# Re-ordering the start of a four-layer residual chain: table loads, corner matrices and low-rank tables

## The chip, the cores and the metric

The kernel runs on one core of a Trainium2 chip. The metric is the device time of one execution in microseconds (us). The kernel before took 628.57 us, the median of three runs (627.66 to 631.0). Engines are named as the profile names them: PE is TensorE, PEld its weight loads, DVE VectorE, ACT ScalarE, POOL GpSimd, SP SyncE; ACTq and SPq are the instruction queues of ACT and SP, which issue DMAs and load registers.

## The reference

The input `x` has 8 batches of 256 tokens of 1024 features. Four residual layers follow each other (all float32):

```python
x = x + _L0_cond_ref(x, W0, b0, coeff, mask)      # x @ W0.T + b0 + coeff[b] * (x @ (2*mask[b]-1))
x = x + _L1_cond_ref(x, w1, scale_log, codebook, lora_A, lora_B)
        # delta = lora_B @ lora_A * 0.5;  n = (w1 + delta) / exp(scale_log) per group of 128 columns
        # q = nearest of 8 codebook levels (7 thresholds);  w_eff = q * scale + delta;  x @ w_eff.T
x = x + _L2_cond_ref(x, tok2, W2, b2, lora_As, lora_Bs)   # x @ W2.T + b2 + 2 * (x @ A[tok2[b]]) @ B[tok2[b]]
x = x + _L3_cond_ref(x, A3, B3, tok3)                     # (x @ B3[tok3[b]].T) @ A3[tok3[b]].T
```

Layers 1 and 2 are linear and the same for every batch, so the kernel multiplies their matrices once: P = (I + W1_eff)^T (I + W2)^T. The low-rank parts become small matrices: V = (I + W2)^T B3^T, and tables G that hold, per batch, the rows that close the product.

## The kernel before

The work has two parts. The first, up to about 232 us, builds P; the second runs eight batches with it. Every float32 matrix is split into a high and a low part (`_hi`, `_lo`, type fp32r), and a product is three matmuls: hi by hi, hi by lo, lo by hi. ACT writes the high part out of PSUM, DVE subtracts it to give the low part.

**Preparation.** SP loads W2 in eight row blocks (`w2n`, line 248). DVE adds the unit matrix to each (`w2_eye`, L795), PE transposes the blocks (L1013), ACT and DVE split them (L536 and L802). After each block PE adds that block's part of V (`v_part`, L1021) into the banks of delta1. Then come the transposes of B2, the small product of B3 and B2 (L1059, L1060), the transposes of A3 (L1066), and the correction of the G tables (L1073, and on DVE L841, L848, L850). POOL does two gathers and the sums of the quantiser.

**Table loads.** The tables of layers 2 and 3 are picked by token numbers. SP runs a loop of eight (L251 to L253): load the number from DRAM into a register, issue a DMA. ACT does the same eight times in its own program (`load_a3`, L523 and L524), two of them ahead of the first scaling of W1.

**Quantisation and P, in eight groups.** A group is 128 columns of W1 in two halves of 128x512. Each half goes through:

- `add_delta` on DVE (L732): raw weight plus the PE product delta (L982);
- `norm` on ACT (L487): division by the scale;
- `terms` on DVE (L740 seven times and L759 once): seven comparisons;
- `sums` on POOL (L405 four times and L407): adding up the comparisons;
- `scaled` on ACT (L473), `effective` on DVE (L771), the split `w1_hi` on ACT (L494) and `w1_lo` on DVE (L775).

PE then computes the group's rows of P: eight steps t, each with three column pieces n (512, 512 and 256 columns) of three matmuls (L1122 to L1124). ACT and DVE split the result (`p_hi` L504 and L509, `p_lo` L785 and L789). In group g, DVE does `terms(g+1,1)`, `add_delta(g+2,0)`, `effective(g+1,0)`, `w1_lo(g+1,0)`, `add_delta(g+2,1)`, `terms(g+2,0)`, `effective(g+1,1)`, `p_lo(g)`, `w1_lo(g+1,1)`. The order on each engine is that of its program; nothing re-orders it. PE also transposes a block of W0 in each group (L998), whose unit matrix POOL has added (L413), and SP stores it.

**Batches.** From about 236 us on, PE runs layer 0 (L1156 to L1158) and the product with P (L1174 to L1176) for the eight batches.

## Time and profile before

| quantity | value |
|---|---|
| median of three runs | 628.57 us (627.66 to 631.0) |
| span of the profiled execution | 627.8 us |
| PE busy in the span | 579.3 us (92%) |
| DVE busy | 403.0 us (64%) |
| ACT busy | 285.2 us (45%) |
| POOL busy | 139.5 us (22%) |
| mean granted TensorE clock | 0.973 of full |

The three runs are timed apart from the profiled execution. Its own time is known only as its span, from the first instruction to the last; the median lies 0.8 us above it. A time in the rows is counted from the start of the span. In the windows each engine's figure is busy time in that stretch, and PEclk is the granted clock as a share of 2.4 GHz.

### The profile page before, as it was taken

Reading aid. Unit: us, or ns where it says so; the run is one execution under the profiler, and the core shown is the slowest. Engines: PE = TensorE matmul, PEld = TensorE weight load, DVE = VectorE, ACT = ScalarE, POOL = GpSimd, SP = SyncE. Lnnn points to the kernel's source line nnn. Section 1 sums busy time; section 2 is a strip of 40 time slices with the busy share of each in tenths; the row PEclk is TensorE's granted clock in tenths of the full one; section 3 lists DMA queues with packets and bytes.
Section 4 is the critical chain, followed back from the end, with each engine's and each line's share of the span. In section 5 each row is a group of like instructions: output and inputs, shape, how many; then the busy total and the mean of one; then the engine's idle time right before and its main releaser. Section 6 shows DMA issues by size and latency. Waiting matters only on the chain.

```text
span 627.8 us, 10523 instructions
## 1 busy us (share of the span) xinstructions
PE 579.3 (92%) x3636; PEld 523.5 (83%) x3636; DVE 403.0 (64%) x591; ACT 285.2 (45%) x535; POOL 139.5 (22%) x133
## 2 busy tenths in 40 slices
PE   5478869988997999999999999999999999999997
PEld 4478658877886889889989989989989988988986
DVE  5585997999999367476466456555646637547621
ACT  1325544344533376555365455455544635545520
POOL 2350576878777210000000000000000000000000
PEclk9579998998998999999999999999999999999999
DMA  8751344133310898128126325414604703803301
GB/s 247 183 94 18 35 135 140 63 100 100 100 33 34 278 351 275 69 101 290 46 101 218 116 96 166 173 57 164 214 33 138 263 19 127 286 3 131 105 1 67
DMA packets 60791, 81.12 MB, mean 129 GB/s; under 512 B 24992, under 2 KB 41376, under 8 KB 60768
## 3 DMA queue, kind: packets, MB, share of 16 engines
q1 hardware_dynamic: 51872, 79.23, 38.6%
q10 hardware_dynamic: 8608, 0.53, 0.9%
q0 software_dynamic: 288, 1.05, 0.4%
q8 instruction: 14, 0.23, 0.2%
q14 instruction: 9, 0.07, 0.0%
HBM read 66.12 MB, written 14.68 MB: 129 GB/s over the span
## 4 chain that ended last, share of the span: by engine, by line
PE 72%; DVE 10%; DMA 6%; issue 4%; ACT 3%; ACTq 2%; SPq 2%; DVEq 0%; POOL 0%; POOLq 0%
PE delta L1174 9%; PE delta L1176 9%; PE delta L1175 9%; PE bank L1156 7%; PE bank L1158 7%; PE bank L1157 7%; PE bank L1122 3%; PE bank L1123 2%; PE bank L1124 2%; PE delta L1158 2%; PE delta L1157 2%; PE delta L1156 2%; ACTq L523 2%; DVE term_b L740 2%; DMA g_dram<-a_lo 2%
## 5 line engine op out<-in xcount | busy, mean ns | idle before, releaser
L609 ACT CAST m_hi<-merged_ring 128x512 fp32r<-128x512 f32 x128 | 77.2, 618 | 86.9 <-PE delta L1158 33.0
L1156 PE MATMUL bank<-x_t_hi,m_hi 128*128 128x256 f32 x384 | 108.8, 283 | 1.9 <-DVE C_lo L789 1.2
L896 DVE TENSOR_TENSOR m_lo<-merged_ring,m_hi 128x512 fp32r<-128x512 f32 x128 | 84.7, 689 | 37.8 <-ACT m_hi L609 37.8
L1158 PE MATMUL bank<-x_t_hi,m_lo 128*128 128x256 f32 x384 | 108.7, 283 | 0.0
L1157 PE MATMUL bank<-x_t_lo,m_hi 128*128 128x256 f32 x384 | 108.7, 283 | 0.0
L1174 PE MATMUL delta<-P_hi,x_t_hi 128*128 128x512 f32 x256 | 101.8, 398 | 0.0
L1176 PE MATMUL delta<-P_hi,x_t_lo 128*128 128x512 f32 x256 | 99.9, 390 | 0.0
L1175 PE MATMUL delta<-P_lo,x_t_hi 128*128 128x512 f32 x256 | 99.8, 390 | 0.0
L890 DVE TENSOR_TENSOR merged_ring<-merged_ring,w_t 128x1024 f32<-128x1024 f32 x64 | 77.1, 1223 | 31.2 <-ACT merged_ring L599 26.3
L599 ACT ACTIVATE merged_ring<-mask_ring,batch_now 128x1024 f32<-128x1024 int32 x64 | 78.0, 1240 | 16.3 <-DMA mask_ring<-in_mask_Bx4096x_ik 15.4
L447 POOL CAST c_batch<-C_hi 128x256 fp32r (+1 forms) x24 | 9.6, 435 | 339.5 <-PE delta L1183 321.1
L1122 PE MATMUL bank<-w_hi 128*128 128x512 f32 (+1 forms) x192 | 72.4, 377 | 6.0 <-DVE P_lo L785 4.8
L1156 PEld LDWEIGHTS bank<-x_t_hi,m_hi 128*128 128x128 f32 x384 | 73.7, 192 | 2.5 <-DVE C_lo L789 1.4
L1157 PEld LDWEIGHTS bank<-x_t_lo,m_hi 128*128 128x128 f32 x384 | 73.7, 192 | 0.3
L1158 PEld LDWEIGHTS bank<-x_t_hi,m_lo 128*128 128x128 f32 x384 | 73.7, 192 | 0.0
L1123 PE MATMUL bank<-w_lo,w_hi 128*128 128x512 f32 (+1 forms) x192 | 69.8, 363 | 0.0
L1124 PE MATMUL bank<-w_hi,w_lo 128*128 128x512 f32 (+1 forms) x192 | 69.5, 362 | 0.0
L405 POOL TENSOR_TENSOR pooled<-pooled,term_b 128x512 f32<-128x512 f32 x32 | 49.1, 1535 | 59.5 <-DVE term_b L740 58.0
L1176 PEld LDWEIGHTS delta<-P_hi,x_t_lo 128*128 128x128 f32 x256 | 48.1, 188 | 10.4
L1175 PEld LDWEIGHTS delta<-P_lo,x_t_hi 128*128 128x128 f32 x256 | 48.2, 188 | 9.0
L1174 PEld LDWEIGHTS delta<-P_hi,x_t_hi 128*128 128x128 f32 x256 | 48.1, 188 | 9.0
L1122 PEld LDWEIGHTS bank<-w_hi 128*128 128x128 f32 x192 | 37.5, 195 | 12.5 <-issue 6.7
(139 smaller groups left out, 995.0 us busy)
## 6 DMA issues: line engine op xcount, KB each, us to landing
mask_ring<-in_mask_Bx4096x_ik SPq DMA_DIRECT2D x64, 512.0 KB, 4.3
w_nat<-in_L_cond_W SPq DMA_DIRECT2D x16, 512.0 KB, 5.4
x_nat<-in_x SPq DMA_DIRECT2D x8, 1024.0 KB, 6.7
out<-out_staged SPq DMA_DIRECT2D x32, 256.0 KB, 2.0
w_raw<-in_L_cond_weight SPq DMA_DIRECT2D x16, 256.0 KB, 3.0
w0t_dram<-w_out SPq DMA_DIRECT2D x8, 512.0 KB, 3.0
w_t<-w0t_dram SPq DMA_DIRECT2D x8, 512.0 KB, 4.8
g_batch<-g_dram SPq DMA_DIRECT2D x32, 128.0 KB, 3.7
```

The lines of the kernel that those rows point to most:

```text
L599: nc.scalar.activation(ring_f[:, k % MR], ring_i[:, k % MR], ACT.Identity, bias=now[:, 1:2], scale=now[:, 0:1]).then_inc(s["s_set"], 1)
L609: nc.scalar.copy(Mh[:, n % MR], ring_f[:, k % MR, h * HALF:(h + 1) * HALF]).then_inc(s["h_set"], 1)
L896: nc.vector.tensor_tensor(Ml[:, n % MR], ring_f[:, k % MR, h * HALF:(h + 1) * HALF], Mh[:, n % MR].bitcast(F32), ALU.subtract).then_inc(s[ ...
L1122: mm(o, W1h[:, t], Wh[:, t, c0:c1], start=(t == 0), stop=False)
L1123: mm(o, W1h[:, t], Wl[:, t, c0:c1], start=False, stop=False)
L1124: ins = mm(o, W1l[:, t], Wh[:, t, c0:c1], start=False, stop=(t == KT - 1))
L1156: mm(dst, mh, xTh[:, k], start=(k == 0 and o % 2 == 0), stop=False, skip_group_check=True)
L1157: mm(dst, mh, xTl[:, k], start=False, stop=False, skip_group_check=True)
L1158: ins = mm(dst, ml, xTh[:, k], start=False, stop=(k == KT - 1), skip_group_check=True)
L1174: mm(o, x1h[:, k, toks], Ph[:, k, cols], start=(k == 0), stop=False)
L1175: mm(o, x1h[:, k, toks], Pl[:, k, cols], start=False, stop=False)
L1176: mm(o, x1l[:, k, toks], Ph[:, k, cols], start=False, stop=False)
```

## The change

The change leaves the batches as they are and rewrites the first part.

- SP loads codebook and scales first, and the wait between W2 blocks 1 and 2 is gone. All sixteen table loads stand on SP in straight code, after the second W1 block and the first W0 block; the token number is read from the SBUF tile `tok` (before: from DRAM). They stand ahead of `raw_next(0, 2, h)`, the third W1 block.
- The unit matrices of W2 are added by POOL; those of W0 are a matmul of `ident` by `ident` on PE. POOL also makes the low part of A2 (`Wl[..D:D+NBR]`) and the low parts of the G tables.
- V no longer sits in the delta banks but in banks 7 and 2, and comes after the 512-column pieces n = 0 and 1 of group 0. Piece 2 of group 0 follows V. The transposes of W2 use three banks in turn instead of four.
- W1 of groups 0 and 2 is split into buffers of its own (`W1h_early`, `W1l_early`), so that `w1_hi` of groups 1 and 2 waits for less.
- The work for A3 and the G tables moves behind group 1 on PE (`tables()`), and behind `terms(3,1)` on DVE (`gsum`).
- The first three group bodies are written out by hand on DVE, ACT and PE, and the hardware loops over groups become straight code.

On DVE, ahead of the hardware loop of groups, the rows of the kernel before are these (`b_nat` is the B2 table, `a_nat` A2, `a_t` A3 transposed, `w_norm` the normed half of W1):

```order
L740 TENSOR_SCALAR term_d<-w_norm,thresholds,steps 128x512
L740 TENSOR_SCALAR term_b<-w_norm,thresholds,steps 128x512
L841 TENSOR_TENSOR b_nat<-b_nat,bank 128x512
L845 TENSOR_TENSOR w_lo<-a_nat,w_hi 128x8x128
L841 TENSOR_TENSOR b_nat<-b_nat,bank 128x512
L848 TENSOR_TENSOR a_lo<-a_t,a_hi 128x1024
L850 SCALAR_TENSOR_TENSOR ga_lo<-b_nat,ga_hi 128x1024
L873 UNCONDITIONAL_BRANCH
```

The terms above it are `terms(1,0)`. In the changed kernel only the two sums on `b_nat` are left on DVE, three groups later, behind `p_lo(1)` and `terms(3,1)`:

```order
L821 TENSOR_TENSOR P_lo<-bank,P_hi 128x512 x2
L825 TENSOR_TENSOR C_lo<-bank,C_hi 128x256
L763 TENSOR_SCALAR acc<-w_norm,thresholds,steps 128x512
L763 TENSOR_SCALAR term_a<-w_norm,thresholds,steps 128x512
L763 TENSOR_SCALAR pooled<-w_norm,thresholds,steps 128x512
L763 TENSOR_SCALAR term_b<-w_norm,thresholds,steps 128x512
L787 SCALAR_TENSOR_TENSOR acc<-acc,codebook_rows,term_a 128x512
L763 TENSOR_SCALAR term_c<-w_norm,thresholds,steps 128x512
L763 TENSOR_SCALAR term_d<-w_norm,thresholds,steps 128x512
L763 TENSOR_SCALAR term_b<-w_norm,thresholds,steps 128x512
L892 SCALAR_TENSOR_TENSOR b_nat<-b_nat,bank 128x512 x2
```

On PE the two products that feed these sums stand ahead of group 0 in the kernel before (`a_t` by `b_b_t`, L1073):

```order
L1066 MATMUL bank<-ident,a_nat 128x128 x8
L1073 MATMUL bank<-a_t,b_b_t 128x512 x2
L989 MATMUL delta<-ident 128x128
L982 MATMUL delta<-lora_a,lora_b_t 128x128 x8
L1122 MATMUL bank<-w_hi 128x512
```

In the changed kernel they stand between groups 1 and 2, and group 2 (the rows with `w_hi_early`) is behind them; the second product waits for the first sum on DVE:

```order
L1112 MATMUL bank<-w_hi,w_lo 128x256
L1153 MATMUL bank<-ident,a_nat 128x128 x8
L1161 MATMUL bank<-a_t,b_b_t 128x512 x2
L1028 MATMUL delta<-ident 128x128
L1021 MATMUL delta<-lora_a,lora_b_t 128x128 x8
L1110 MATMUL bank<-w_hi,w_hi_early 128x512
```

The diff, cut to its core:

```diff
 # sync
+            for h in range(2):
+                raw_next(0, 1, h)      # (b2c and the first block of W0 follow)
+            sp.wait_ge(s["tok_in"], 32)
+            for b in range(NB):
+                slot = sp.value_load(tok[0:1, 0, b:b + 1], min_val=0, max_val=a2.shape[0] - 1)
+                sp.dma_start(a2n[:, :, b, :], a2_rows[bass.ds(slot, 1)]...).then_inc(s["a2_in"], 16)
+            for b in range(NB):
+                slot = sp.value_load(tok[0:1, 1, b:b + 1], min_val=0, max_val=a3.shape[0] - 1)
+                sp.dma_start(a3n[:, :, b, :], a3_rows[bass.ds(slot, 1)]...).then_inc(s["a3_in"], 16)
+            for h in range(2):
+                raw_next(0, 2, h)
...
+            group(0, True, True)
             sp.wait_ge(s["y_set"], 1)
...
+            group(1, True, True)
+            group(2, True, True)
             sp.wait_ge(s["ga_hi"], 2)      # store of the G tables
 # gpsimd
+            for t in range(5):
+                w2_eye(t)
+            sums(0, 0)
+            for t in range(5, KT):
+                w2_eye(t)
+            sums(0, 1)
+            pool.wait_ge(s["ab_hi"], 1)
+            nc.gpsimd.tensor_tensor(Wl[:, :, D:D + NBR], a2n..., Wh[:, :, D:D + NBR]..., ALU.subtract)
             sums(1, 0)
+            group(0, 2)
+            group(1, 2)
+            group(2, 2)
+            pool.wait_ge(s["ga_hi"], 1)
+            nc.gpsimd.tensor_tensor(a3l[:, :], a3t[:, :], a3h..., ALU.subtract)
+            pool.wait_ge(s["ga_hi"], 2)
+            nc.gpsimd.tensor_tensor(gal[:, :], b2n[:, :], gah..., ALU.subtract)
 # scalar
-            for b in range(W2_FIRST):
-                load_a3(b)
             act.wait_ge(s["scale_set"], 1)
             for h in range(2):
                 norm(0, h, first=True)
...
+            w1_hi(2, 0)
+            p_hi(0, range(2))
+            w0_evac(0, 0, first=True)
+            p_hi(0, range(2, 3))
+            norm(3, 1)
+            w0_evac(0, 1, first=True)
+            scaled(2, 1)
+            w0_evac(1, 0)
+            w1_hi(2, 1)
+            w0_evac(1, 1)
+            p_hi(1)
+            a3_set(0)
 # vector
+            terms_a(0, 0, first=True, reused=False)   # four comparisons
+            w2_lo(0)
+            terms_b(0, 0)                             # the other four instructions
+            w2_lo(1)
...
+            w2_lo(7)
+            w1_lo(0, 1)
+            terms(1, 0)
+            terms(1, 1)
+            add_delta(2, 0, 0)
+            effective(1, 0, 1)
+            w1_lo(1, 0)
+            add_delta(2, 1, 0)
+            terms(2, 0)
+            effective(1, 1, 1)
+            w1_lo(1, 1)
+            v_lo(0)
+            terms(2, 1)
+            v_lo(1)
+            add_delta(3, 0, 1)
+            effective(2, 0, 0)
+            w1_lo(2, 0)
+            add_delta(3, 1, 1)
+            p_lo(0, range(2))
+            dve.wait_ge(s["bb_done"], 1)              # then b3b2 and y_col
+            terms_a(3, 0)
+            p_lo(0, range(2, 3))
+            terms_b(3, 0)
+            effective(2, 1, 0)
+            w1_lo(2, 1)
+            p_lo(1)
+            def group(g, par, quant, tables=False):
                 if quant:
                     terms(g + 1, 1)
+                if tables:                            # g == 2
+                    for h in range(2):
+                        gsum(h)
 # tensor
+            pe.wait_ge(s["w2_lo"], 2 * KT)
+            for n in range(2):
+                for t in range(KT):
+                    comp(n, t, *w1_split(0))          # pieces 0 and 1 of group 0
+            for k in range(HT):
+                v_part(k)
+            eye(2, 0)
+            delta(3, 1)
+            for k in range(HT, KT):
+                v_part(k)
+            pe.wait_ge(s["v_lo"], 1)                  # then the product of B3 and B2
+            pe.wait_ge(s["v_lo"], 2)
+            pe.wait_ge(s["ab_lo"], 1)
+            for t in range(KT):
+                comp(2, t, *w1_split(0))
+            pe.wait_ge(s["b3b2_set"], 1)
+            w0_transpose(0, 0, first=True)            # then group 1
+            tables()
+            def tables():
+                ...                                   # eight transposes of A3
+                for h in range(2):
+                    if h == 0:
+                        pe.wait_ge(s["a3_set"], 2)
+                    else:
+                        pe.wait_ge(s["gsum_set"], 1)
+                    mm(bank[MISC][:, :], b3b2[:, :], a3t[:, h * 512:(h + 1) * 512], start=True, stop=True)
```

## Rows read from the trace of the kernel before

**Rows 1.** Windows: stretch, its length, busy us (instructions) by engine, PEclk, DMA share, GB/s.

```profile
93.30:98.40 5.10, 5.07 (x18) 4.52 (x19) 4.97 (x9) 2.52 (x8) 3.30 (x3) 0.50 0.78 243
133.20:153.00 19.80, 17.04 (x98) 14.82 (x98) 18.43 (x26) 8.64 (x25) 15.43 (x12) 1.00 0.25 80
232.00:627.80 395.80, 391.83 (x2555) 358.42 (x2553) 221.94 (x319) 190.17 (x293) 10.03 (x28) 1.00 0.38 132
```

**Rows 2.** Chain that ended last, `effective` on DVE in two groups: start, us.

```profile
133.17 0.67 DVE acc L771
...
153.04 0.69 DVE acc L771
```

**Rows 3.** Timeline of PE, group 3: start, us, operation, idle before and releaser.

```profile
129.81 0.39 PE L989 MATMUL delta<-ident 128*128 128x128 f32 x2
...
133.90 1.16 PE L982 MATMUL delta<-lora_a,lora_b_t 128*128 x8 [2.82 <-DVE acc L771]
134.82 0.47 PE L1122 MATMUL bank<-w_hi 128*128 128x512 f32 x1
...
149.66 0.39 PE L989 MATMUL delta<-ident 128*128 128x128 f32 x2
```

**Rows 4.** Timeline of ACT before the first scaling.

```profile
14.09 6.93 ACTq L524 DMA_DIRECT2D a_nat<-in_L_cond_A  x2
...
21.36 2.44 ACT L487 ACTIVATE w_norm<-w_norm,scale_recip_now 128x128 f32<-128x128 f32 x8
```

**Rows 5.** Timeline of DVE in the preparation.

```profile
12.03 1.27 DVE L732 TENSOR_TENSOR w_norm<-w_raw,delta 128x512 f32<-128x512 f32 x2
...
22.67 0.55 DVE L740 TENSOR_SCALAR acc<-w_norm,thresholds,steps 128x512 f32<-128x512 f32 x1 [8.09 <-ACT w_norm L487]
...
31.20 2.47 DVE L802 TENSOR_TENSOR w_lo<-bank,w_hi 128x512 fp32r<-128x512 f32 x4
33.60 0.53 DVE L740 TENSOR_SCALAR acc<-w_norm,thresholds,steps 128x512 f32<-128x512 f32 x1
...
39.35 1.55 DVE L795 TENSOR_TENSOR w_nat<-w_nat,ident 128x128 f32<-128x128 f32 x2
...
64.30 0.54 DVE L740 TENSOR_SCALAR acc<-w_norm,thresholds,steps 128x512 f32<-128x512 f32 x1
```

**Rows 6.** Timeline of DVE, steady groups.

```profile
133.77 1.28 DVE L785 TENSOR_TENSOR P_lo<-bank,P_hi 128x512 f32 x2
...
136.40 1.32 DVE L740 TENSOR_SCALAR acc<-w_norm,thresholds,steps 128x512 f32<-128x512 f32 x1
...
143.14 0.68 DVE L732 TENSOR_TENSOR w_norm<-w_raw,delta 128x512 f32<-128x512 f32 x1
...
145.68 0.69 DVE L775 TENSOR_TENSOR w_lo<-acc,w_hi 128x512 fp32r<-128x512 f32 x1 [1.26 <-ACT w_hi L494]
```

**Rows 7.** Timeline of DVE: comparison c with POOL idle, then with POOL adding.

```profile
99.00 0.53 DVE L740 TENSOR_SCALAR term_c<-w_norm,thresholds,steps 128x512 f32<-128x512 f32 x1
...
109.98 1.51 DVE L740 TENSOR_SCALAR term_c<-w_norm,thresholds,steps 128x512 f32<-128x512 f32 x1
```

**Rows 8.** POOL's sums (L405), all: min/median/max ns.

```profile
L405 POOL TENSOR_TENSOR pooled<-pooled,term_d x16: 1261/1336/1367, 28.4 to 202.9; 128x512 f32<-128x512 f32 x16
```

**Rows 9.** Table loads on SP (L252, L253), ns.

```profile
L252 SPq TENSOR_LOAD <-in_itok_B_ptr x8: 930/1032/1837, 12.2 to 38.2; - x8
L252 SPq TENSOR_LOAD <-in_itok_B x8: 473/514/915, 14.2 to 39.4; - x8
L253 SPq DMA_DIRECT2D a_nat<-in_L_cond_lora_As x8: 387/389/3810, 15.7 to 40.4; - x8
```

**Rows 10.** Timeline of PE: V in the preparation; after its longest wait in the groups.

```profile
26.74 5.63 PE L1021 MATMUL delta<-b_t,w_nat 128*128 128x128 f32 x32 [7.76 <-ACT b_t L541]
...
93.33 2.05 PE L982 MATMUL delta<-lora_a,lora_b_t 128*128 128x128 f32 x8 [5.42 <-DVE acc L771]
```

**Rows 11.** Loads of W0 blocks 1 to 7 on SP (L290).

```profile
DMA to landing us min/median/max: 3.5/4.0/5.6
```

More of the change, by code:

```diff
@@ L547, in _ @@
-            for h in range(2):
-                act.wait_ge(s["prep_done"], V0 + h + 1)
-                nc.scalar.copy(Wh[:, h * HT:(h + 1) * HT, D + NBR:EXT], bank[VBANK[h]][:, :]).then_inc(s["prep_hi"], 1)
-            for h in range(2):
-                act.wait_ge(s["prep_done"], B2T0 + h + 1)
-                nc.scalar.copy(b2t[:, h * HT:(h + 1) * HT, :], bank[0 + h][:, :]).then_inc(s["prep_hi"], 1)
-            scaled(0, 1, first=True)
-            for h in range(2):
-                w1_hi(0, h, first=True)
@@ L557, in _ @@
-            for h in range(2):
-                norm(1, h)
-            for h in range(2):
-                act.wait_ge(s["prep_done"], A3T0 + h + 1)
-                nc.scalar.copy(a3t[:, h * 512:(h + 1) * 512], bank[h][:, :]).then_inc(s["prep_hi"], 1)
+            w2_hi(0)
+            w2_hi(1)
+            b3_set(0)
+            w2_hi(2)
+            b3_set(1)
+            w2_hi(3)
+            b2_set(0)
+            w2_hi(4)
+            scaled(0, 0, first=True)
+            b2_set(1)
+            w2_hi(5)
@@ L572, in group, with v_hi, a3_set @@
-            def group(g, quant, first=False):
+            def v_hi(h):
+                act.wait_ge(s["v_done"], h + 1)
+                nc.scalar.copy(Wh[:, h * HT:(h + 1) * HT, D + NBR:EXT], bank[VBANK[h]][:, :]).then_inc(s["v_hi"], 1)
+            def a3_set(h):
+                act.wait_ge(s["a3_tr"], h + 1)
+                nc.scalar.copy(a3t[:, h * 512:(h + 1) * 512], bank[MISC][:, :]).then_inc(s["a3_set"], 1)
+            scaled(1, 0)
+            norm(2, 0)
+            w1_hi(1, 0)
+            norm(2, 1)
@@ new lines, in _, with group @@
+            scaled(1, 1)
+            w1_hi(1, 1)
+            v_hi(0)
+            scaled(2, 0)
+            v_hi(1)
+            norm(3, 0)
+            w1_hi(2, 0)
[10 more added lines that the diff above has]
+            a3_set(0)
+            def group(g, quant, tables=False):
@@ L581, in group @@
                     norm(g + 2, 1)
+                if tables:
+                    act.wait_ge(s["gsum_set"], 2)
+                    nc.scalar.copy(gah[:, :], b2n[:, :]).then_inc(s["ga_hi"], 1)
                 if quant:
                     scaled(g + 1, 1)
-                w0_evac(g, 1, first)
-                p_hi(g, first)
+                w0_evac(g, 1)
+                p_hi(g)
                 if quant:
                     w1_hi(g + 1, 1)
-            group(0, 2, first=True)
-            group(1, 2)
-            with act.Fori(1, (G - 2) // 2) as j:
-                group(2 * j, 2)
-                group(2 * j + 1, 2)
+            for g in range(2, G - 2):
+                group(g, 2, tables=(g == 2))
             group(G - 2, 1)
@@ L826, in _ @@
-            for h in range(2):
-                effective(0, h, 0)
-            for h in range(2):
-                w1_lo(0, h)
+            terms_a(0, 0, first=True, reused=False)
+            w2_lo(0)
+            terms_b(0, 0)
+            w2_lo(1)
+            terms_a(0, 1, reused=False)
+            w2_lo(2)
+            terms_b(0, 1)
+            w2_lo(3)
+            w2_lo(4)
+            effective(0, 0, 0)
+            w2_lo(5)
+            w1_lo(0, 0)
+            w2_lo(6)
             for h in range(2):
@@ L868, in group @@
                     w1_lo(g + 1, 1)
-            per = 2 * 2 * 2
-            pairs = (G - 2) // 2
-            start = step.n
-            with dve.Fori(0, pairs) as j:
-                step.rebase(start + j * per)
-                group(2 * j, 0, 2)
-                group(2 * j + 1, 1, 2)
-                assert step.n == per, step.n
-            step.rebase(start + pairs * per)
+            for g in range(2, G - 2):
+                group(g, g % 2, 2, tables=(g == 2))
             dve.wait_ge(s["late_in"], 32)
@@ L1027, in _, with b3_transpose @@
[L1027 to L1031 removed]
+                        ins = nc.tensor.transpose(bank[W2RING[i % 3]][:, j * P:(j + 1) * P], w2n[:, t, k * P:(k + 1) * P], ident[:, :])
+                    ins.then_inc(s["w2_tr"], 1)
+            def b3_transpose(h):
+                if h == 0:
+                    pe.wait_ge(s["b3_in"], 16)
+                else:
+                    pe.wait_ge(s["b3_set"], 1)
@@ L1046, in _, with b2_transpose @@
-            pe.wait_ge(s["prep_lo"], 2 * KT)
-            for h in range(2):
+                    ins = nc.tensor.transpose(bank[MISC][:, t * P:(t + 1) * P], b3n[:, k * P:(k + 1) * P], ident[:, :])
+                ins.then_inc(s["b3_tr"], 1)
+            def b2_transpose(h):
+                if h == 0:
+                    pe.wait_ge(s["b2_in"], 16)
+                    pe.wait_ge(s["b3_set"], 2)
+                else:
+                    pe.wait_ge(s["b2_set"], 1)
                 for t in range(HT):
@@ L1087, in x_transpose, with group @@
                 ins.then_inc(s["t_done"], 1)
-            COLS = [(0, 512), (512, 1024), (1024, EXT)]
-            def group(g, par, quant, first=False, last=False):
+            def group(g, par, quant, last=False):
                 if quant:
```

420 lines of the change are left out of this document (197 added, 223 removed).

## The prediction

> **What bounds the kernel now.** I read the windows first, then the chain that ended last, then the timelines of PE, DVE, ACT and POOL up to 235 us, and at the end the queues. The windows show two regimes. From 232 us on PE is busy 391.8 of 395.8 us at full clock [rows 1]. The change does not touch this part, so it can only move its start. In a steady group, PE is busy 17.0 of 19.8 us and DVE 18.4. The chain agrees: `effective` of two groups lies at 133.17 and 153.04, 19.87 us apart, both pieces on DVE [rows 2], and PE stands 2.82 us before the delta of group 3 for exactly this DVE step [rows 3]. A group of PE work takes 149.66 - 134.82 = 14.8 us; a group of DVE work takes 19.9 us. So the groups are bound by DVE, in program order, and what counts is when DVE gets through the preparation, unless PE becomes late.
>
> The first comparison starts at 22.67, after 8.09 us of waiting for ACT [rows 5]. ACT could not scale because two table loads stood in front in its program (14.09 to 21.02); it scales from 21.36 [rows 4]. The terms of group 1 start at 64.30.
>
> **Part by part.** I follow DVE through the changed order, and PE where DVE has to wait for it. Times count from the span's start.
>
> *Step 1, the first comparison.* The first half of `add_delta` ends at 12.03 + 0.64 = 12.67. From the first scaling to the first comparison it took 22.67 - 21.36 = 1.3 us, and a small copy stands ahead (estimate 0.2). So terms(0,0) starts at about 14.2 instead of 22.67: 8.5 us earlier. The moved queue entries cost nothing here: codebook and scales come before the LoRA matrices, which land about 1 us later, and PE's first delta has that much room before DVE's chain of small operations is through.
>
> *Step 2, up to terms(1,0).* DVE has two passes of terms at 39.35 - 33.60 = 5.75 us each, 16 low parts of W2 at 2.47 / 4 = 0.62 (9.9), and six PSUM or split operations at 0.62 (3.7) [rows 5]. That is 25.1 us. The eight unit matrices are gone from DVE (one pair took 1.55). Each of the two splits of W1 waits for ACT 1.26 us [rows 6]: 2.5. So terms(1,0) starts at 14.2 + 25.1 + 2.5 = 41.8, against 64.30. In the kernel before V, its copies and the third transposes of PE lay between; they are now hidden behind terms of groups 1 and 2. The unit matrices on POOL delay its first sum, but W2 has landed by then; at worst they cost one POOL addition, 1.3 us [rows 8].
>
> *Step 3, up to the product of B3 and B2 being picked up (about 82.9).* Four passes of terms: 5.75 us when POOL rarely collides, 143.14 - 136.40 = 6.74 in a steady group [rows 6]. I take 6.5, since POOL is adding all the time: 26.0. POOL makes the low part of A2 ahead of sums(1,0): twice the size of a sum of 1.34, so 2.5 to 2.7 us in which the last comparison waits; I take 2.5 (none to 4 are the ends, since the DVE version in the kernel before was not in POOL's way). Four `add_delta`, three `effective`, three `w1_lo`, two `v_lo` at 0.62 and a pair of P_lo of 1.28: 8.7. Two waits for `w1_hi`: 2.5. The third, `w1_hi(2,0)`, waits for piece 2 of group 0, and that waits for V: after `effective(1,1)` PE does half a delta, 32 matmuls of V (5.63 us, partly at low clock, [rows 10]), the small product and half of piece 2, about 12 us, while DVE has 10.5 us to do. So 1.5 us. The sum is 41.2, and y_col is there at about 83.0.
>
> *Step 4, group 1 on PE.* It cannot start before that, because bank 7 holds the product. A transpose of W0 stands ahead (0.4), the group takes 14.8, the third piece waits for C_lo behind four comparisons (0.7), and step t = 3 needs the second block of W0, which is only requested after the second transpose: 0.4 + 4.0 us of landing [rows 11] against two steps of 1.8 us, so 0.8. It ends at about 99.9 (with the unit-matrix matmuls, 0.2, at 100.1). DVE has nothing left to do meanwhile: `p_lo(1)` stands in its order, and terms(3,1) is queued behind it. After ACT's 0.6 and 1.6 us of P_lo and C_lo, terms(3,1) starts at 102.3, with the sums of POOL long done, and takes about 6.3: 108.6.
>
> *Step 5, the G tables.* This is the wait the change adds. The second product of `tables()` waits for the first `gsum`, which DVE does after terms(3,1). Group 2 and all of PE is queued behind it. gsum 0.6, product 0.6: 109.8. PE stood for some 5 us. After a wait of 5.42 us the trace shows the next 5.1 us at a granted clock of 0.50, 1.2 GHz [rows 1, 10]. The delta then takes 1.7 us more to the first matmul of the group, and the group loses half of the remaining 3.4: 109.8 + 1.9 + 14.8 + 1.7 = 128.2. P_hi (0.6, of which 0.35 lies beside the last piece): P_lo(2) starts at 128.4.
>
> *Step 6, from there on.* Before, P_lo(2) started at 133.77 [rows 6]. The lead is 5.4 us. DVE would have been there at about 121, so PE is what is late. Afterwards DVE's 19.9 us per group bound again, and PE's 14.8 plus delta has room. POOL's a3l and gal (2.6 us each) fit into the gap before P_lo(2). The unit matrix of W0 leaves POOL: it touches one comparison per group, I take 0.15 us each, 0.5 in all; the extra unit matmuls in the last two groups, where PE bounds, give 0.3 back. Dynamic loops into straight code: the group before and after the loop's end have the same 19.9 us, so nothing. Sum: 5.6 us.
>
> The sum stands against the profiled execution of 627.8: 622.2. The median lies 0.8 above the span, so 628.57 - 5.6 = 623.0.
>
> *A rule against the change.* Comparison c took 0.53 us with POOL idle and 1.51 with POOL adding [rows 7]; the difference, 0.98, stays below one POOL addition (1.34). The Trainium skill (SBUF — State Buffer, "SBUF: two separate sides") says that VectorE and GpSimd share a port pair as an exclusive lock, held for a whole instruction; the trace agrees with 1.51 us. By that rule three subtractions of 1024 columns on POOL each hold DVE for up to 2.6 us, where DVE's own cost was 1.7 to 2.3, and the move would gain nothing. By the order above two of the three fall into DVE's gap.
>
> **Rivals.**
> *A longer lead (617.5).* Step 3 is pessimistic where POOL and DVE miss each other: with all six comparisons passes at 5.3 us (eight instructions, one collision instead of two) the passes save 4 x 1.2 + 2 x 0.45 = 5.7 us, and all of it reaches group 1 on PE. For it: sums(0,0) starts early. Against it: steady groups show 6.7.
> *Nothing left (627.5).* The lead is eaten by PE: group 1 also begins at 1.2 GHz (1.7), the second W0 block lands in 5.6 us instead of 4.0 (1.6) [rows 11], and the late A2 part holds DVE 1.3 more: 4.6 us, so 627.6. For it: PE stands before group 1 as well, for a few us.
> *Slower (641).* The sixteen table loads stand on SP ahead of the third W1 block, which `add_delta(2,0)` needs at 41.8 + 13.0 + 2.5 = 57.3. SP comes to them at about 15. The trace has no register load from SBUF. From below: a load of the value, 0.51, a DMA issue, 0.39, and register work of 0.6, 1.5 us each: done at 39. From above: the loop before took 12.2 to 40.8 for eight, 3.6 us each, with the pointer load of 1.03 and DMA issues up to 3.81 [rows 9]: done at 72.2, landed at 75.6, 18.3 us late, 641.3. It decides above (57.3 - 15 - 3.4) / 16 = 2.4 us per table. I take 1.5, since the pointer load is gone and W2 has landed after the first few.
> The Trainium skill (Runtime: NRT & Kernel Launch, "The ~15µs preamble/postamble breakdown") gives about 1.3 us for a register load from HBM; the trace shows 0.51 and 1.03. By 1.3 us a table costs 2.3, just inside.
>
> **How the numbers follow.** Forecast (620 to 626): 45%. Longer lead (613 to 620): 22%. Nothing left (626 to 630): 20%. Slower by the table loads: 8%. Other late steps adding up beyond 630: 5%. A measurement can tell about 0.5%, 3.1 us: faster is below 625.4, slower above 631.7. Faster: 22% and nine tenths of 45%, 0.63. Same: 0.22. Slower: 0.15. The range, 615 to 631, leaves out a part of the longer lead and the slower cases; the forecast's own range is 620 to 626.
>
> **What would show it.** First comparison near 14; terms(1,0) near 42; y_col near 83; PE with a wait of about 5 us before the second product of `a_t`, and PEclk 0.50 after it; P_lo(2) waiting for PE and starting near 128; later groups 19.9 us apart on DVE; layer 0 starting near 230. I am wrong if `add_delta(2,0)` waits for a DMA, if P_lo(2) does not wait for PE, or if DVE's period is no longer 19.9.

## The result and the profile after

The changed kernel takes 642.3 us (median of 5 runs, 638.0 to 642.6) against 628.7 of the kernel before: ratio 1.018, 95% interval 1.015 to 1.021. The whole interval lies above 1: it is slower, by 1.8%. I had forecast 623.0 us. The profiled execution is the quickest of the five (638.0, span 636.2). A later comparison gave the unaltered kernel 638.8 us (ratio 1.013, 1.007 to 1.019), so the loss is 10 to 14 us.

The windows after, columns as in [rows 1]:

```profile
90.00:108.70 18.70, 17.50 (x97) 14.53 (x98) 8.99 (x16) 7.57 (x20) 6.67 (x5) 1.00 0.58 128
108.70:135.40 26.70, 21.86 (x107) 17.69 (x108) 16.17 (x25) 9.72 (x24) 11.24 (x8) 0.87 0.21 67
135.40:158.60 23.20, 18.50 (x113) 16.24 (x112) 21.74 (x25) 9.39 (x27) 19.19 (x13) 0.98 0.33 106
178.40:198.30 19.90, 16.94 (x97) 14.48 (x96) 18.44 (x27) 8.64 (x25) 14.97 (x11) 1.00 0.16 54
240.00:636.00 396.00, 391.13 (x2547) 357.55 (x2545) 221.04 (x318) 189.40 (x292) 10.04 (x28) 1.00 0.38 132
```

In the batches PE is as busy as it was (391.1 of 396.0 us), and a steady group is still 19.9 us with 17 of PE and 18.4 of DVE. The loss lies in two stretches. Group 2 (108.7 to 135.4) takes 26.7 us with DVE busy only 16.2, so DVE waits there for 10.5. The next (135.4 to 158.6) takes 23.2 with DVE busy 21.7, so there DVE has more to do or does it more slowly.

The starts of the same steps in six kernels, from their timelines (us; `effective` and the P_lo of each group are on DVE; the four on the right are experiments of the next section):

| start of | before | after | g1 | g3 | h1 | i2 |
|---|---|---|---|---|---|---|
| effective(1,0) | 83.2 | 61.0 | 60.8 | 61.6 | 61.0 | 73.7 |
| P_lo(0) | 93.3 | 88.5 | 88.1 | 86.2 | 85.6 | 83.6 |
| P_lo(1) | 113.9 | 107.1 | 108.0 | 106.0 | 104.0 | 103.5 |
| P_lo(2) | 133.8 | 135.4 | 131.0 | 129.0 | 127.1 | 123.4 |
| P_lo(3) | 153.6 | 159.1 | 150.6 | 151.0 | 147.9 | 143.2 |
| P_lo(6) | 210.4 | 217.2 | 207.5 | 209.0 | 206.0 | 201.0 |
| P_lo(7) | 226.8 | 233.8 | 224.1 | 225.6 | 222.6 | 217.3 |
| span | 627.8 | 636.2 | 627.8 | 627.5 | 626.5 | 619.5 |

Read the first two columns downwards. The new order is 22.2 us ahead at effective(1,0), 4.8 at P_lo(0), 6.8 at P_lo(1), and then behind: 1.6, 5.5, 6.8, 7.0, and 8.4 in the span.

The timeline of PE after (start, us, operation, idle before and releaser) shows the first part of this:

```profile
56.07 7.30 PE L1082 MATMUL bank<-b_t,w_nat 128*128 128x128 f32 x64
...
71.01 2.08 PE L1021 MATMUL delta<-lora_a,lora_b_t 128*128 128x128 f32 x8 [5.32 <-DVE acc L803]
72.88 8.69 PE L1082 MATMUL bank<-b_t,w_nat 128*128 128x128 f32 x64
...
90.18 0.30 PE L1037 MATMUL bank<-ident,w_nat 128*128 128x128 f32 x1 [2.16 <-DVE b_b_t L880]
...
110.48 1.13 PE L1161 MATMUL bank<-a_t,b_b_t 128*128 128x512 f32 x2 [1.23 <-ACT a_t L568]
115.21 2.07 PE L1161 MATMUL bank<-a_t,b_b_t 128*128 128x512 f32 x2 [3.60 <-DVE b_nat L892]
```

Half of V is 32 matmuls in the code and stands here as x64. The row of before, x32 in 5.63 us, was therefore 16 matmuls and not the 32 that I read in it [rows 10]. The last row is the wait that the change adds: the second product of the tables, 3.60 us behind the first sum on DVE, and after it the clock has fallen:

```profile
115.20:120.20 5.00, 4.99 (x17) 3.96 (x18) 1.33 (x3) 0.00 (x0) 3.02 (x3) 0.50 0.00 0
```

The granted clock is 0.50, that is 1.2 GHz, for the 5 us from the product on, and the product takes 2.07 us where its twin took 1.13.

ACT and DVE in the same stretch, one fence each:

```profile
102.70 0.59 ACT L517 COPY w_out<-bank 128x512 f32<-128x512 f32 x1 [7.40 <-DMA w0t_dram<-w_out]
103.18 0.62 ACT L496 CAST w_hi_early<-acc 128x512 fp32r<-128x512 f32 x1
...
124.90 0.59 ACT L517 COPY w_out<-bank 128x512 f32<-128x512 f32 x1 [13.39 <-PE bank L1037]
125.38 0.21 ACT L483 COPY scale_recip_now<-scale_recip 128x8 f32<-128x8 f32 x1
125.62 1.28 ACT L488 ACTIVATE w_norm<-w_norm,scale_recip_now 128x128 f32<-128x128 f32 x4
126.81 0.61 ACT L496 CAST w_hi<-acc 128x512 fp32r<-128x512 f32 x1
```

```profile
117.32 0.69 DVE L892 SCALAR_TENSOR_TENSOR b_nat<-b_nat,bank 128x512 f32<-128x512 f32 x1 [2.16 <-PE bank L1161]
119.55 0.69 DVE L758 TENSOR_TENSOR w_norm<-w_raw,delta 128x512 f32<-128x512 f32 x1 [1.54 <-PE delta L1021]
120.16 0.68 DVE L803 TENSOR_TENSOR acc<-pooled,delta 128x512 f32<-128x512 f32 x1
127.45 0.69 DVE L808 TENSOR_TENSOR w_lo<-acc,w_hi 128x512 fp32r<-128x512 f32 x1 [6.61 <-ACT w_hi L496]
...
135.37 1.38 DVE L821 TENSOR_TENSOR P_lo<-bank,P_hi 128x512 fp32r<-128x512 f32 x2 [0.21 <-ACT P_hi L506]
...
139.04 2.61 DVE L763 TENSOR_SCALAR term_a<-w_norm,thresholds,steps 128x512 f32<-128x512 f32 x1
141.58 2.62 DVE L763 TENSOR_SCALAR pooled<-w_norm,thresholds,steps 128x512 f32<-128x512 f32 x1
144.12 0.53 DVE L763 TENSOR_SCALAR term_b<-w_norm,thresholds,steps 128x512 f32<-128x512 f32 x1
```

Twice ACT stands at the copy of a W0 column block, once for the store of the block before (7.40 us) and once for PE's transpose (13.39), and behind it in ACT's order stands the split of W1 for which DVE waits. The second time DVE stands for 6.61 us; with 2.16 at the second sum and 1.54 at `add_delta` that makes 10.3 of the 10.5 us. P_lo(2), where I had expected the wait, has 0.21: PE's group 2, which it needs, runs from the second product at 115.21 to 135.7 without a wait, so DVE and PE come to P_lo(2) at the same time. Then two comparisons take 2.6 us instead of 0.54; POOL's timeline has its two low parts exactly there:

```profile
138.80 2.57 POOL L432 TENSOR_TENSOR a_lo<-a_t,a_hi 128x1024 fp32r<-128x1024 f32 x1
141.34 2.58 POOL L434 TENSOR_TENSOR ga_lo<-b_nat,ga_hi 128x1024 fp32r<-128x1024 f32 x1
```

The table loads on SP did what they were meant to (16 loads in 18.3 us, answering to [rows 9]; the raw data of group 2 are asked for at 42.26):

```profile
23.94 8.68 SPq L252 DMA_DIRECT2D a_nat<-in_L_cond_lora_As  x8
33.41 8.81 SPq L255 DMA_DIRECT2D a_nat<-in_L_cond_A  x8
42.26 1.71 SPq L242 DMA_DIRECT2D w_raw<-in_L_cond_weight  x2
```

### The profile page after: what moved, and what is told of

The parts are those of the page before. It is cut to its first block, busy times and chain, and to the rows that moved or that the text cites. A ratio compares the mean times of both kernels' runs of the same rounds, so it can differ in the third digit from the quotient of the medians.

```text
span 636.2 us, 10123 instructions
## 1 busy us (share of the span) xinstructions
PE 585.6 (92%) x3652; PEld 527.0 (83%) x3652; DVE 401.7 (63%) x580; ACT 285.6 (45%) x535; POOL 143.3 (23%) x136
## 4 chain that ended last, share of the span: by engine, by line
PE 76%; DVE 11%; DMA 2%; ACT 2%; issue 1%; DVEq 0%; ACTq 0%
PE delta L1258 9%; PE delta L1260 9%; PE delta L1259 9%; PE bank L1240 7%; PE bank L1242 7%; PE bank L1241 7%; PE bank L1110 4%; PE bank L1112 3%; PE bank L1111 3%; PE delta L1242 2%; PE delta L1241 2%; PE delta L1240 2%; DVE term_b L763 2%; DVE term_c L763 1%; PE bank L1082 1%; PE delta L1267 1%
## 5 line engine op out<-in xcount | busy, mean ns | idle before, releaser
L1242 PE MATMUL bank<-x_t_hi,m_lo 128*128 128x256 f32 x384 | 108.7, 283 | 0.0
L1241 PE MATMUL bank<-x_t_lo,m_hi 128*128 128x256 f32 x384 | 108.7, 283 | 0.0
L625 ACT ACTIVATE merged_ring<-mask_ring,batch_now 128x1024 f32<-128x1024 int32 x64 | 77.9, 1239 | 19.2 <-DMA mask_ring<-in_mask_Bx4096x_ik 18.4
L1240 PEld LDWEIGHTS bank<-x_t_hi,m_hi 128*128 128x128 f32 x384 | 73.7, 192 | 3.9 <-DVE m_lo L934 2.3
L1241 PEld LDWEIGHTS bank<-x_t_lo,m_hi 128*128 128x128 f32 x384 | 73.7, 192 | 0.3
L1242 PEld LDWEIGHTS bank<-x_t_hi,m_lo 128*128 128x128 f32 x384 | 73.7, 192 | 0.0
L1110 PE MATMUL bank<-w_hi 128*128 128x512 f32 x144 | 55.0, 382 | 4.6 <-DVE P_lo L821 4.6
L406 POOL TENSOR_TENSOR pooled<-pooled,term_b 128x512 f32<-128x512 f32 x32 | 46.8, 1464 | 48.9 <-DVE term_b L763 46.2
L1260 PEld LDWEIGHTS delta<-P_hi,x_t_lo 128*128 128x128 f32 x256 | 48.0, 188 | 10.4
L1111 PE MATMUL bank<-w_lo,w_hi 128*128 128x512 f32 x144 | 52.9, 368 | 0.0
L1112 PE MATMUL bank<-w_hi,w_lo 128*128 128x512 f32 x144 | 52.8, 367 | 0.0
L959 DVE TENSOR_TENSOR out_staged<-delta,b_rows 128x512 f32<-128x512 f32 x32 | 21.4, 688 | 38.4 <-PE delta L1274 38.4
```

The lines of the kernel that those rows point to most:

```text
L625: nc.scalar.activation(ring_f[:, k % MR], ring_i[:, k % MR], ACT.Identity, bias=now[:, 1:2], scale=now[:, 0:1]).then_inc(s["s_set"], 1)
L1110: mm(o, hi[:, t], Wh[:, t, c0:c1], start=(t == 0), stop=False)
L1111: mm(o, hi[:, t], Wl[:, t, c0:c1], start=False, stop=False)
L1240: mm(dst, mh, xTh[:, k], start=(k == 0 and o % 2 == 0), stop=False, skip_group_check=True)
L1241: mm(dst, mh, xTl[:, k], start=False, stop=False, skip_group_check=True)
L1242: ins = mm(dst, ml, xTh[:, k], start=False, stop=(k == KT - 1), skip_group_check=True)
```

## The experiments

Each comparison ran beside the kernel before: 630.2 us in the first (e), 629.1 in the second (g), 628.7 in the third (h), 629.2 in the fourth (i). The changed kernel itself ran again only in the second (g0, 638.8 us); the e and h runs are set against it by their ratios. Marks such as P_lo(2) are those of one profiled execution each. The theory at the start: the loss is two waits by queue order in group 2 and the collision on POOL. The rivals: V is simply longer than I took it, or PE's clock is the limit.

**e1, the second product of the tables two tiles into group 2.**

```
-  (tables) wait gsum_set >= 1; matmul(b3b2, a3t[512:])
+  (group 2, t == 2) wait gsum_set >= 1; matmul(b3b2, a3t[512:])
   (as before)       wait gsum_set >= 2; transpose of W0
```

> The changed kernel with one edit: the second product of the G tables moves from the front of group 2 to just ahead of the first W0 transpose of group 2 (step t = 2), so PE does eye, delta and two steps of group 2 while DVE does terms(3,1). Theory A (that wait is what makes PE, then ACT and then DVE late): PE no longer stands 3.6 us at 115.2, w1_hi(3,0) no longer waits behind the W0 copy until 126.8, DVE's wait of 6.6 us before w1_lo(3,0) falls under 1, and P_lo(2) starts near 128 to 129 instead of 135.4: 6 to 7 us less, ratio to the kernel before about 1.008 (from 1.018). Theory B (PE is late anyway, by group 1 and by V before it, and the wait costs only itself): 2 us or less, ratio 1.015 or more.

636.0 us (631.0 to 639.5, 7 runs), ratio 1.009 (1.006 to 1.012). The wait of DVE at `w1_lo(3,0)` shrinks from 6.61 to 2.32 and P_lo(2) comes 5.5 us earlier:

```profile
121.94 0.69 DVE L808 TENSOR_TENSOR w_lo<-acc,w_hi 128x512 fp32r<-128x512 f32 x1 [2.32 <-ACT w_hi L496]
...
129.85 1.38 DVE L821 TENSOR_TENSOR P_lo<-bank,P_hi 128x512 fp32r<-128x512 f32 x2 [0.20 <-ACT P_hi L506]
```

The profiled execution is the fastest of the seven. In the medians the gain over g0 is smaller (ratio 1.009 against 1.013) and the intervals overlap; the same holds for e2.

**e2, the low parts of the G tables left out** (the high parts are stored twice).

```
-  gpsimd a3l = a3t - a3h (1024 columns), gal = b2n - gah (1024 columns)
+  gpsimd the same on 8 columns; store (gah, a3h) twice
```

> The changed kernel without the low parts of the G tables: POOL's two subtractions of 1024 columns are cut to 8 columns and the high parts are stored twice (this leaves part of the computation out). Theory A (each holds DVE's next comparison for a whole POOL instruction: term_a 2.61 and pooled 2.62 us at 139 instead of 0.54): 4.1 us less, all of it on the path since DVE bounds the groups from there on, ratio about 1.0115. Theory B (the stall only fills time that DVE would wait for PE or ACT): under 1 us, ratio 1.017 to 1.019.

635.0 us (633.1 to 641.6, 10 runs), ratio 1.010 (1.007 to 1.014). From P_lo(2) to P_lo(3) it is 19.6 us instead of 23.7, and comparison a is back at 0.53:

```profile
136.41 1.38 DVE L821 TENSOR_TENSOR P_lo<-bank,P_hi 128x512 fp32r<-128x512 f32 x2 [0.21 <-ACT P_hi L506]
...
140.10 0.53 DVE L763 TENSOR_SCALAR term_a<-w_norm,thresholds,steps 128x512 f32<-128x512 f32 x1
...
156.03 1.28 DVE L821 TENSOR_TENSOR P_lo<-bank,P_hi 128x512 fp32r<-128x512 f32 x2
```

**e3, V in one piece** ahead of `eye(2,0)` and `delta(3,1)`.

```
-  v_part(0..3); eye(2, 0); delta(3, 1); v_part(4..7)
+  v_part(0..7); eye(2, 0); delta(3, 1)
```

> The changed kernel with V computed in one piece: all eight v_part ahead of eye(2,0) and delta(3,1) on PE. Theory A (the second half of V, 8.7 us at half clock behind a delta that waits for DVE, sets piece 2 of group 0 and the pick-up of the B3-B2 product): V ends near 71, the waits of DVE at 82 (2.2 us) and 87 (3.2 us) go, y_col comes near 86 instead of 90, and 3 to 4 us reach the end, ratio about 1.012. Theory B (DVE's own passes of terms set y_col): under 1.5 us, ratio 1.016 or more.

638.7 us (637.2 to 639.9, 4 runs), ratio 1.013: no gain that can be told from the unaltered kernel. y_col comes 3 us earlier (86.97), but P_lo(1) starts at 107.62 (after: 107.10). ACT's copy waits for the store, and PE's second transpose of W0 waits for the copy; one fence each:

```profile
101.66 0.58 ACT L517 COPY w_out<-bank 128x512 f32<-128x512 f32 x1 [9.33 <-DMA w0t_dram<-w_out]
```

```profile
102.30 0.90 PE L1037 MATMUL bank<-ident,w_nat 128*128 128x128 f32 x4 [1.92 <-ACT w_out L517]
```

That is 1.9 us. From this wait to P_lo(1) (102.3 to 107.6) the granted clock is 0.68, where it is 1.00 before P_lo(1) in after and in g2; by my estimate (5.3 us times 0.32) this is another 1.7.

**e4, one part of the change alone:** the kernel before with all sixteen table loads unrolled on SP, numbers read from SBUF, none on ACT.

```
-  sp: Fori over 8 tables, number from HBM        act: load_a3(b) between the copies
+  sp: for b in 0..7 load a2, for b in 0..7 load a3, number from tok in SBUF
```

> The kernel before with one part of the change: all sixteen table loads on SP in straight code with the token read from SBUF, none on ACT. Theory A (the 8 us of DVE waiting for the first scaling is on the path up to the groups): first comparison near 14 instead of 22.7, everything behind it about 8 us earlier, 620 to 621 us, ratio 0.987. Theory B (another chain is bound to come through at the old time: V and the transposes on PE, or the stores of the G tables before P_hi(0)): 0 to 3 us, ratio 0.995 to 1.0.

621.4 us (618.8 to 623.7, 4 runs), ratio 0.984 (0.979 to 0.988): faster than both kernels.

**g0, the changed kernel once more.**

> The changed kernel unaltered, beside the others. Its first profiled execution had 638.0 us and the other four 640.5 to 642.6. Theory A: what is wrong with it is fixed by its order, so the marks repeat (P_lo(2) at 135.4, effective(3,1) at 158.5), and the execution is between 638 and 643, the scatter coming from the granted clock of the stretch before 230 us. Theory B: the profiled one was a lucky case and P_lo(2) comes as much as 4 us later here.

638.8 us (637.0 to 639.2, 4 runs). P_lo(2) at 136.8, effective(4,1) at 159.9. (In the expectations of the g comparison the step called effective(3,1) is this one; I had counted it wrongly.) P_lo(2) and effective(4,1) repeat within 1.5 us, P_lo(1) does not: 109.45 instead of 107.10. Here PE did wait for the copy behind the store, which it did not in the first profile:

```profile
105.69 0.66 PE L1037 MATMUL bank<-ident,w_nat 128*128 128x128 f32 x4 [1.75 <-ACT w_out L517]
```

**g1, e1 and e2 together** (low parts left out as in e2).

> Two edits at once: the second product of the tables stands two tiles into group 2, and the low parts of the G tables are left out (the high part is stored twice). Alone they gave 636.0 and 635.0 us against 642.3. Theory A: they are two separate losses (the DVE waiting at group 2 for ACT and TensorE; POOL's low parts locking out DVE in group 3), so the gains add: P_lo(2) at 129.9, P_lo(3) at 149.5, the last P_lo at about 224, span 625 to 626, median 627 to 630. Theory B: both only shorten one shared wait, and the median stays at 634 to 636.

629.7 us (627.4 to 632.7, 10 runs), ratio 1.001 (0.998 to 1.004). 9.1 us less than g0, so together the two are most of the 10 us. In the marks they add: P_lo(2) is 4.3 us earlier than in after, and P_lo(3), at 150.61, another 4.1.

**g2, V in one piece and a buffer of its own for W0's block 1.**

```
+  w0_alt = 4 KB in the region of ga_lo (free until group 3)
-  copy of block 1 to w0_out, after the store of block 0
+  copy of block 1 to w0_alt, without that wait; store from w0_alt
+  gal on POOL waits for that store
```

> V in one piece, and the W0 columns of group 1 leave TensorE's bank for a buffer of their own, so that ScalarE needn't wait for the store of group 0 (9.3 us in the trace with V in one piece). Theory A: V in one piece started group 1 about 3 us earlier and the wait for the store ate it; without the wait group 1 ends at about 103.5 instead of 107.0, w1_lo(2,1) has no wait over 1 us, and all later marks are 3 to 4 us earlier: median 634 to 636. Theory B: the wait stands beside another one (the product of the tables, DVE) and group 2 starts when it did: 638 to 640.

635.1 us (633.2 to 636.6, 10 runs), ratio 1.009 (1.006 to 1.011): 3.7 less than g0 beside it, and the two ranges don't meet. P_lo(1) starts at 104.42 instead of e3's 107.62, and the granted clock of group 1 is 1.00. So with V in one piece the wait for the store was what held group 1. The buffer without the change to V was not run; by PE's waits in the two profiles of the unaltered kernel it should give between nothing (after) and 1.8 us (g0). My figure for `w1_lo(2,1)` was wrong: 2.64 us of wait remain, for PE's transpose.

**g3, all of it mended, nothing left out:** e1, e3, the buffer, the two low parts on DVE at the end of group 2, and terms(3,1) ahead of P_lo(1) on DVE.

```
-  dve: w1_lo(2,1); p_lo(1); terms(3,1); gsum ...      pool: a3l, gal
+  dve: w1_lo(2,1); terms(3,1); p_lo(1); gsum ... w1_lo(3,1); a3l; gal
```

> The changed kernel with V in one piece, the buffer of its own for W0, the second product of the tables two tiles into group 2, the low parts of the G tables on VectorE at the end of group 2 (all computed, nothing left out), and the terms (3,1) ahead of P_lo(1) on VectorE. Theory A (the loss sits in queue order, not in the work): P_lo(1) has no wait on VectorE, P_lo(2) comes at 122 to 125 and the period is 19.9 from there but for 2.4 us of low parts, so the last P_lo is at 218 to 221: median 620 to 625. Theory B (TensorE at half clock in V and the work on it are what limits, whatever the order): P_lo(2) not before 128 and a median of 627 or more.

628.6 us (626.4 to 630.0, 10 runs), ratio 0.998 (0.995 to 1.001). 10.2 less than g0 and level with the kernel before. These are theory B's numbers: P_lo(1) has almost no wait on DVE (0.87), as A said, but P_lo(2) is at 128.98. DVE now waits at the two sums for PE's products:

```profile
110.51 0.69 DVE L891 SCALAR_TENSOR_TENSOR b_nat<-b_nat,bank 128x512 f32<-128x512 f32 x1 [2.83 <-PE bank L1162]
116.87 0.69 DVE L891 SCALAR_TENSOR_TENSOR b_nat<-b_nat,bank 128x512 f32<-128x512 f32 x1 [5.66 <-PE bank L1162]
```

**h1, g3 with the second sum behind `w1_lo(3,0)`** on DVE, and `w1_hi(3,0)` ahead of the W0 copy on ACT.

> The kernel with all five mendings (628.6 us), and in group 2 VectorE takes the second G-table sum behind w1_lo(3,0) instead of ahead of effective(3,0); ScalarE takes w1_hi(3,0) ahead of the W0 columns. In the trace of the five mendings VectorE stood 5.66 us in front of that sum. Theory A (TensorE's group 2, 15 us long and begun at 110, is what P_lo(2) waits for next): VectorE's wait only moves to P_lo(2), which comes at 127 to 129 as before (128.98), and the median is 627 to 629. Theory B (VectorE's order alone sets it): P_lo(2) at 124, median 623 to 625.

627.3 us (626.1 to 630.2, 10 runs), ratio 0.997 (0.995 to 0.999). As theory A said, the wait only moves, to P_lo(2):

```profile
114.93 0.69 DVE L894 SCALAR_TENSOR_TENSOR b_nat<-b_nat,bank 128x512 f32<-128x512 f32 x1 [1.84 <-PE bank L1166]
...
127.05 1.38 DVE L822 TENSOR_TENSOR P_lo<-bank,P_hi 128x512 fp32r<-128x512 f32 x2 [4.43 <-ACT P_hi L504]
...
129.28 1.22 DVE L920 TENSOR_TENSOR a_lo<-a_t,a_hi 128x1024 fp32r<-128x1024 f32 x1
130.41 1.22 DVE L921 TENSOR_TENSOR ga_lo<-b_nat,ga_hi 128x1024 fp32r<-128x1024 f32 x1
```

**h2, h1 with terms(4,1) ahead of P_lo(2)** on DVE, and `w1_hi(3,1)` ahead of the second W0 copy on ACT.

> As the one with the later sum, and VectorE takes the terms (4,1) ahead of P_lo(2), with w1_hi(3,1) ahead of the W0 columns on ScalarE. Theory A (VectorE, 19.9 us of work a group, is the bound as soon as nothing queued in it waits): effective(4,0) comes at 134 to 136 instead of 141.0, the last P_lo at about 219, median 621 to 624. Theory B (the order can't give that back, because TensorE then waits for P_lo(2)): 627 to 629.

630.2 us (627.4 to 631.5, 10 runs), ratio 1.001: 2.9 more than h1, against theory A. effective(4,0) comes at 139.8, not 134 to 136 (h1: 138.0). DVE did not wait; what it had in hand became slower, and PE stood for the late P_lo(2), as theory B said (with 627 to 629 us, which was too low); DVE, then PE:

```profile
134.89 2.20 DVE L925 TENSOR_TENSOR a_lo<-a_t,a_hi 128x1024 fp32r<-128x1024 f32 x1
137.01 2.30 DVE L926 TENSOR_TENSOR ga_lo<-b_nat,ga_hi 128x1024 fp32r<-128x1024 f32 x1
```

```profile
134.19 0.47 PE L1123 MATMUL bank<-w_hi 128*128 128x512 f32 x1 [3.02 <-DVE P_lo L824]
```

The same two subtractions took 1.22 us each in h1, with POOL idle; here POOL is adding.

**h3, half of V's matmuls left out.**

```
-  for t in range(8): V += w2n[t] x b3t[t]
+  for t in range(4): V += w2n[t] x b3t[t]
```

> The changed kernel with V summed over half of its tiles (half of V's matmuls left out), which gives V the 8 us that the prediction took for all of it. Theory A (the 7 us that y_col and group 1 came late were not what cost the time: the store of the W0 columns and the product of the tables stand behind it): y_col at 82 to 84 instead of 89.9, but P_lo(1) only 2 to 3 us earlier than 107 to 109, and a median of 635 to 638 against 638.8 of the changed kernel in the last comparison. Theory B (V's length is the loss): everything from y_col on is 7 us earlier, median 631 to 633.

639.2 us (637.8 to 639.3, 4 runs), ratio 1.016: not below g0's 638.8 at all. y_col came at 87.1, 2.8 us earlier and not 7; PE's wait for DVE between the halves of V stays (4.20 us). That lead is gone before P_lo(1) (109.15): PE waits 1.87 us at the same transpose, and the granted clock of group 1 is 0.67 from 87.1 to 92.2 and 0.68 from 103.8 to 109.2. The store, seen from DVE:

```profile
104.34 0.69 DVE L808 TENSOR_TENSOR w_lo_early<-acc,w_hi_early 128x512 fp32r<-128x512 f32 x1 [9.85 <-ACT w_hi_early L496]
```

**h4, the kernel before with only the first table's loads unrolled.**

> The kernel before, with only the loads of the first table unrolled on the sync queue with their numbers read from SBUF; the loads of the second table stay on ScalarE's queue. With both tables moved the kernel before gained 8.8 us (621.4 against 630.2). Theory A (what counts is that ScalarE no longer issues and reads numbers while VectorE waits for its first scaling): little is gained here, 627 to 630. Theory B (what counts is the faster reading on the sync queue, so that the first columns' raw data and W2 come earlier): half or more of the 8.8 us is gained, 621 to 626.

630.5 us (628.1 to 633.2, 10 runs), ratio 1.004 (1.001 to 1.006). In the profiled execution, the fastest of the ten, the first comparison is at 19.44 and P_lo(7) at 221.45, 5.3 earlier than before, yet the span is only 1.4 shorter, and the median of all ten is 1.9 longer than before. Of the 3.9 us that were lost behind P_lo(7), 2.5 are PE's wait in layer 0, 3.18 us where it was 0.71 before (row of PE); the granted clock of 0.83 from 230 to 240 us is about 1.7 more (estimate, 10 us times 0.17):

```profile
233.02 0.39 PE L1157 MATMUL bank<-x_t_hi,m_hi 128*128 128x256 f32 x1 [3.18 <-DVE m_lo L897]
```

**i1, only the second table's loads taken off ACT.**

> The kernel before, with only the eight loads of the second table taken off ScalarE and put on the sync queue behind the first table's, numbers read from SBUF; the first table stays in its loop with numbers read from HBM (25.1 us for eight). Theory A (the gain of moving both is ScalarE's freed queue: the first scaling no longer waits): the first comparison comes at 14 to 15 instead of 22.7, the last P_lo at 217 to 220, median 620 to 624. Theory B (it takes both, since the raw data of group 2 now stand behind 25 us of loop and 9 of loads and come 5 us later): raw data late, median 626 or more.

624.1 us (623.5 to 624.9, 4 runs), ratio 0.993 (0.990 to 0.996). First comparison at 15.11, and the price that theory B named is there as well, but smaller than the gain:

```profile
55.43 0.69 DVE L727 TENSOR_TENSOR w_norm<-w_raw,delta 128x512 f32<-128x512 f32 x1 [3.36 <-DMA w_raw<-in_L_cond_weight]
```

**i2, both tables' loads on SP, as e4.**

> The kernel before with both tables' loads on the sync queue, once more, beside the one with a single table moved. Theory A: 619 to 624 again (it had 618.8 to 623.7 in four runs). Theory B: the four runs were lucky in the granted clock, and it is 625 to 628.

621.2 us (620.3 to 622.3, 4 runs), ratio 0.988 (0.985 to 0.991). The gain of e4 repeats. Its rows on SP:

```profile
12.70 17.50 SPq L254 DMA_DIRECT2D a_nat<-in_L_cond_lora_As  x8
30.96 8.74 SPq L257 DMA_DIRECT2D a_nat<-in_L_cond_A  x8
```

## Why the prediction was wrong

I forecast P_lo(2) 5.4 us ahead of before; it came 1.6 behind, and 3.8 more were lost in the next group. Three terms of the sum failed: DVE's wait for POOL in step 2, the size of V in step 3, and POOL's low parts in step 6, which I had put at nothing and which measured 4.1 us. A fourth, the wait for the store, is in no step.

*Step 1 held.* First comparison at 13.28 us (14.2 said):

```profile
13.28 0.55 DVE L763 TENSOR_SCALAR acc<-w_norm,thresholds,steps 128x512 f32<-128x512 f32 x1 [0.52 <-ACT w_norm L488]
```

i1 shows that this, ACT freed of the loads, is worth 5 us by itself.

*Step 2 was 1.9 us late.* terms(1,0) at 43.74 (41.8 said), though the first comparison was 0.9 early. "W2 has landed by then; at worst they cost one POOL addition, 1.3 us" was wrong: POOL adds five unit matrices ahead of its first sum, the fifth waits for its W2 block until 19.19, and DVE stands 2.79 us for that sum; POOL, then DVE:

```profile
19.19 0.45 POOL L396 TENSOR_TENSOR w_nat<-w_nat,ident 128x128 f32<-128x128 f32 x1 [0.78 <-DMA w_nat<-in_L_cond_W]
19.60 1.26 POOL L406 TENSOR_TENSOR pooled<-pooled,term_b 128x512 f32<-128x512 f32 x1
```

```profile
20.89 0.55 DVE L763 TENSOR_SCALAR term_b<-w_norm,thresholds,steps 128x512 f32<-128x512 f32 x1 [2.79 <-POOL pooled L406]
```

*Step 3 failed in the size of V.* y_col at 89.93 instead of 83.0. I took 5.63 us as 32 matmuls; it was 16, because the trace lists two records for an f32 matmul of V [rows 10]; h3, whose halves have 16 matmuls each, prints x32 for each. Half of V is 7.3 us at full clock and 8.69 after the wait (granted clock 0.83). Of the 6.9 us that y_col is late, 1.9 come from step 2, and 2.8 go when half of V's matmuls are left out (h3); for the other 2.2 no run shows the cause.

*Step 4 had its length right and one wait too few.* From y_col to the end of group 1 it is 17.4 us (17.1 said, where the single terms add up to 16.9). But I looked only at the landing of W0's second block and not at the store of the first, for which ACT waits 7.40 us. In the first profile PE had no wait from it, since V was late: the 6.4 us that P_lo(1) is late (107.10 against 100.7) were all there at y_col. In g0 it held PE for 1.75 us, and with V shorter it held PE for 1.9 (e3, h3); g2 took both away and gained 3.7.

*Step 5 was right in size and wrong in place.* From terms(3,1) to P_lo(2) I said 26.1 us; it was 108.73 to 135.37, 26.6. I had DVE waiting at P_lo(2). It waits at `w1_lo(3,0)`, because in ACT's order `w1_hi(3,0)` stands behind the W0 copy, this behind PE's transpose, and this behind the second product. I had named PE's queue behind the added wait, and not ACT's. The size does not come from ACT's order, though. PE's wait of 3.60 us and its group 2 behind it set P_lo(2): e1 takes that wait away and P_lo(2) comes 5.5 us earlier, while in h1, where `w1_hi(3,0)` no longer stands behind the copy, the wait only moves to P_lo(2). What ACT's order did was to move the gap away from P_lo(2), where step 6 needed it; that was not tested by itself.

*Step 6 failed, and with it the sum.* "POOL's a3l and gal (2.6 us each) fit into the gap before P_lo(2)": there was no gap there (0.21). DVE did terms(4,0) up to 134.5, POOL came to a3l behind their sums at 138.80, and each low part held one comparison for 2.6 us, 4.1 us together (e2: 19.6 instead of 23.7). The rule of the Trainium skill that I set against my own sum (SBUF — State Buffer, "SBUF: two separate sides", an exclusive lock held for a whole instruction) told this, and the trace agrees: 2.61 and 2.62 us of DVE beside 2.57 and 2.58 of POOL.

The bill at the profiled run, against my 622.2: 7.0 at P_lo(2) (steps 2 and 3, and 0.5 of step 5), 3.8 in the next group (step 6), 1.6 from P_lo(3) to P_lo(7) (the granted clock is 0.82 from 199.0 to 217.2; the like stretch before, 193.4 to 210.4, had 0.90), 1.4 after P_lo(7), and the 0.2 of step 6 that was to come: 14.0.

*The rivals.* Slower by the table loads (641) is refuted although the number came true: a table costs 1.1 us, and `add_delta(2,0)` did not wait. "Nothing left" named the A2 low part, which was there (POOL 2.61 us), and a low clock, which lay in V (PE 8.69 us instead of 7.3) and not in group 1 (1.00); it did not name the store. The 0.05 for "other late steps adding up" was far too little for a change that touches five queues.

*Where the promised gain went.* Not into one place. The change puts V, the small product and the tables' products, which before ran while DVE prepared W2, between the groups of PE. Mended in all points (h1) it still comes out only 1.4 us below before: 22 us of lead at effective(1,0), 9.9 at P_lo(1), 6.7 at P_lo(2), 4.2 at P_lo(7), 1.3 in the span. At P_lo(2) DVE stands 4.43 us for PE there: between the groups PE is late, not DVE. i2 keeps the old order and has 10.4 at P_lo(1) and 8.3 in the span. Which of the moves costs how much of the 22 us was not separated further. Open is also why four of the first five runs of the changed kernel were 2.6 to 4.6 us above the fifth, and all of g0 near the fifth; the wait for the store, which differs between the two profiles of this kernel, is one candidate that no run separated.
